# More identity products of TensorE at the beginning of a fused attention and expert layer, and score steps that carry theirs in the score bank

## What is computed

```
x = x + layernorm(attn(layernorm(x)))        # 16 heads of 8 channels, softmax over 256 keys
x = x + layernorm(ffn(layernorm(x)))
attn(x): q, k, v = split(x @ w_qkv); softmax(q k^T / sqrt(128)) v, heads joined, @ w_out
ffn(x):  logits = x @ Wr + bias; weights = softmax of the two largest of 8
         out = sum over experts of weight * ((silu(x @ Wg[e]) * (x @ Wu[e])) @ Wd[e])
         out = out + (silu(x @ Sg) * (x @ Su)) @ Sd
```

## Time and profile before

| | us |
|---|---|
| median of three executions | 377.91 |
| lowest and highest | 376.65 and 379.62 |
| profiled execution, its own time | 378.36 |
| span of its trace, first to last instruction | 376.6 |
| TensorE busy in the span | 347.9 |
| VectorE busy | 312.3 |
| ScalarE busy | 268.8 |
| GpSimd busy | 200.2 |

### The profile page before, as it was taken

The page is one execution under the profiler, slowest core; times in us unless marked ns, Lnnn a source line. Parts: engine busy times, 40 slices in busy tenths (PEclk is TensorE's granted clock), DMA queues, the critical chain, the costliest instruction groups (busy, mean ns, idle before and its releaser), DMA issues.

```text
span 376.6 us, 9905 instructions
## 1 busy us (share of the span) xinstructions
PE 347.9 (92%) x3230; PEld 220.5 (59%) x3230; DVE 312.3 (83%) x788; ACT 268.8 (71%) x511; POOL 200.2 (53%) x518
## 2 busy tenths in 40 slices
PE   6986898899999999999998999999999999998892
PEld 6854444455465657574756565665665556666672
DVE  8498498978989999998997979989998996767661
ACT  5643668788887886877888887787669868964522
POOL 5623134305372584466666455765355648867644
PEclk9899899999999999999999999999999999999998
DMA  2457946716468466367265574734664241222210
GB/s 83 120 136 159 199 98 160 167 39 151 131 157 184 119 167 156 99 145 184 52 190 119 148 168 128 172 100 132 146 150 107 61 127 58 78 71 73 58 30 29
DMA packets 59921, 45.64 MB, mean 121 GB/s; under 512 B 8966, under 2 KB 56966, under 8 KB 59870
## 3 DMA queue, kind: packets, MB, share of 16 engines
q1 hardware_dynamic: 59870, 45.00, 48.6%
HBM read 26.69 MB, written 17.81 MB: 118 GB/s over the span
## 4 chain that ended last, share of the span: by engine, by line
PE 46%; POOL 15%; issue 13%; DVE 9%; ACT 6%; DMA 6%; SPq 4%; POOLq 1%; DVEq 0%; ACTq 0%
PE pvp L648 9%; PE bank_d L818 7%; PE sc L632 6%; PE bank_d L802 6%; PE sc L617 4%; DVE mx L997 4%; PE bank_d L803 4%; POOL hidden L1206 4%; POOL rstd L1139 3%; PE bank_a L701 3%; DMA qs<-mT 2%; ACT pr L846 2%; PE bank_d L775 1%; SPq L534 1%; DMA rwb<-rw_dram 1%
## 5 line engine op out<-in xcount | busy, mean ns | idle before, releaser
L997 DVE TENSOR_REDUCE mx<-sc 128x4 f32<-128x1024 f32 x128 | 154.0, 1218 | 20.1 <-PE sc L617 18.7
L846 ACT ACTIVATE pr<-sc 128x1024 f32<-128x1024 f32 x128 | 130.5, 1024 | 25.5 <-PE sc L632 24.2
L648 PE MATMUL pvp<-pr,va 128*32 128x256 f32 x1024 | 68.4, 385 | 0.0
L802 PE MATMUL bank_d<-x3T,wg_sb 128*128 128x256 f32 x160 | 54.8, 424 | 3.2 <-DVE hidden L1095 2.8
L632 PE MATMUL sc<-qs,ks 51*128 51x256 bf16 x512 | 50.2, 277 | 6.6 <-DMA qs<-mT 4.3
L617 PE MATMUL sc<-ks,qs 48*128 48x256 bf16 x512 | 49.4, 274 | 3.1 <-DMA ks<-qk_dram 1.0
L1206 POOL TENSOR_TENSOR hidden<-hidden,rwb 128x256 f32<-128x256 f32 x60 | 42.8, 728 | 16.4 <-DMA rwb<-rw_dram 16.4
L803 PE MATMUL bank_d<-x3T,wu_sb 128*128 128x256 f32 x160 | 47.7, 380 | 0.0
L1139 POOL TENSOR_TENSOR rstd<-vareps,mhalf 128x2 f32<-128x2 f32 x64 | 44.5, 695 | 0.0
L929 ACT ACTIVATE th<-bank_d 128x256 f32<-128x256 f32 x80 | 30.4, 382 | 16.7 <-PE bank_d L803 15.7
L648 PEld LDWEIGHTS pvp<-pr,va 128*32 128x32 f32 x1024 | 26.7, 109 | 25.4 <-issue 13.1
(11 more groups left out here) (113 smaller groups left out, 488.6 us busy)
## 6 DMA issues: line engine op xcount, KB each, us to landing
rwb<-rw_dram SPq DMA_DIRECT2D x30, 256.0 KB, 4.3
qk_dram<-parts SPq DMA_DIRECT2D x30, 192.0 KB, 2.6
qs<-qk_dram SPq DMA_DIRECT2D x30, 192.0 KB, 4.6
ks<-qk_dram SPq DMA_DIRECT2D x30, 192.0 KB, 4.9
qk_dram<-parts SPq DMA_DIRECT2D x30, 128.0 KB, 2.6
pv_dram<-pv_sb SPq DMA_DIRECT2D x14, 256.0 KB, 2.3
x_sb<-in_L_attn_x_dram SPq DMA_DIRECT2D x16, 128.0 KB, 2.7
out_dram<-x SPq DMA_DIRECT2D x16, 128.0 KB, 1.9
```

The costliest lines, as they stand in the source:

```text
L648: mm = pe.matmul(pvp[32 * j:32 * j + 32, g, :], values[:, X * c + 4 * g + j, 32 * tt:32 * tt + 32], pr[:, k, c * N:(c + 1) * N], start=(tt ...
L802: pe.matmul(bank_d[bank][:, 0:N], wg_sb[:, ORDER[n], :], x3T[b % 2][:], start=True, stop=True)
L846: nc.scalar.activation(pr[:, 2 * s:2 * s + 2, :].rearrange("p k n -> p (k n)"), sc[PAIR["s2", b, s]][:].rearrange("p u c n -> p (u c n)"), ...
L997: nc.vector.tensor_reduce(mx[b % 2][:, :, :, s].rearrange("p c u -> p u c"), sc[PAIR["s1", b, s]][:], AX.X, ALU.max).then_inc(max_done, 1)
```

## The change

The table `FILL` is rewritten, and a second table `FILL_SCORES` takes all products that stand ahead of score steps. In the old tables there are 39 products, in the new two 38 and 32, together 70, so that by the tables 31 are added. The order of the steps is kept.

What changes beside the numbers is the place. Ahead of a score step the products used to run before every wait of the step, into `bank_d[1]`. Now the step first waits for its score bank (`turn(sc_empty[pair])`), then runs its products into that score bank, then waits for what else it needs (the layout of queries and keys, the maxima), and then runs its own four matmuls over the same bank.

```diff
 FILL = {
-    "maxT": {0: 9},
-    "qk": {0: 1},
-    "s1_3": {0: 2},
-    "s1_4": {0: 2, 1: 1},
-    "s1_5": {0: 2, 2: 1},
-    "s2_0": {0: 2},
-    "s2_4": {0: 2, 1: 1},
-    "s2_5": {0: 1},
-    "sel1": {0: 2},
-    "xT": {0: 12, 3: 1},
+    "maxT": {0: 10, 1: 1}, "qk": {0: 2, 3: 1}, "sel1": {0: 2}, "v": {1: 1, 3: 1}, "xT": {0: 18, 3: 2},
+}
+FILL_SCORES = {
+    ("s1", 0, 3): 2, ("s1", 0, 4): 3, ("s1", 0, 5): 2, ("s1", 1, 0): 4, ("s1", 1, 3): 1, ("s1", 1, 4): 1,
+    ("s1", 2, 5): 1, ("s1", 3, 6): 1, ("s2", 0, 0): 8, ("s2", 0, 4): 2, ("s2", 0, 5): 1, ("s2", 1, 0): 4,
+    ("s2", 1, 2): 1, ("s2", 1, 4): 1,
 }
...
+            def fill_scores(kind, b, s, pair):
+
+                for _ in range(FILL_SCORES.get((kind, b, s), 0)):
+                    pe.matmul(sc[pair][:, 0, 0, 0:P], ident[:], ident[:], start=True, stop=True)
+
             def s1(b, s):
 
+                pair = PAIR["s1", b, s]
+                turn(sc_empty[pair])
+                fill_scores("s1", b, s, pair)
                 if b and s == 0:
                     pe.wait_ge(qk_stacked[b % 2], landed1(4, b))
...
-                pair = PAIR["s1", b, s]
-                turn(sc_empty[pair])
                 q, k = qs[b % RING], ks[:, b % RING]
...
             def s2(b, s):
+                pair = PAIR["s2", b, s]
+                turn(sc_empty[pair])
+                fill_scores("s2", b, s, pair)
                 if s == 0:
                     pe.wait_ge(max_stacked[b % 2], landed(2, b))
                     if b == 0:
                         pe.wait_ge(minus_load, DMA * 2)
-                pair = PAIR["s2", b, s]
-                turn(sc_empty[pair])
```

## The result

The changed kernel takes 383.49 us in the median of four executions (382.95 to 384.67), before 377.28 us beside it; the ratio is 1.0178, 95% interval 1.0133 to 1.0223. Unchanged and run again in another set it took 384.56 us against 378.49, ratio 1.0164 (1.0122 to 1.0207). I had forecast 375.5 us, in a range of 373.7 to 378.8. A ratio counts only executions within 1.5% of the fastest of their kernel, while a median is of all of them; since before spreads from 371.9 to 385.7 us, it loses many of its slower ones, and a ratio can be nearer to one than the medians beside it.

The account below looks back on a forecast made before the run. Three falls of TensorE's clock behind idle time were taken as all that added products could win, at most 5.1 us. Terms -1.4 - 1.05 - 1.3 + 1.1 = -2.65 us gave a forecast of 375.5 us, range 373.7 to 378.8.

Parts of the forecast that it names:

- Part 4: Products moved behind the wait on a busy bank, at score steps: costs 1.1 us in sum, bounds 0 and 1.5.
- Part 2: First-pass scores to maxT, batch 0 beside batches 1 and 3: added products fit or are covered, cost 0, else 0.4 us.
- part 3: Eight products ahead of s2_0 of batch 0: cost 0, bound 0.2; kept-up clock gains 1.05 us, bounds 0 and 1.7.
- Part 1: Products added ahead of the first transposition and qk: cost 0, other bound 1.1 us; clock gain 1.4 us, bounds 0 and 1.7.
- Part 5: Third fall of the clock, 73 to 78 us: it goes too, gaining 1.3 us, bounds 0 and 1.7.
- Carried rigidly to the end: From some 80 us on, no product added and order unchanged: whatever is won or lost by then reaches the end unaltered.
- The slower rival: Three low clock stretches remain before 80 us, at other places, and part 4's delays stay: 379.5 us, chance 0.10.

Follow-up runs that it names:

- e6: e1 with twelve products ahead of the first transposition and one ahead of the first qk, as before the change; 374.52 us, ratio 0.9973 to before.
- e8: e6 unaltered, run again for a second trace; 374.61 us, ratio 0.9932 to before.
- e1: Changed kernel, all 70 products kept, those ahead of score steps back in bank_d[1] ahead of every wait; 379.60 us, ratio 1.001 to before.
- e3: Changed kernel with twelve products ahead of the first transposition and one ahead of the first qk, as before; 379.82 us, ratio 1.0062 to before.
- e4: Changed kernel without its products behind busy banks; 376.54 us, ratio 0.9972 to before.
- after again: The changed kernel unaltered, run again for a second trace; 384.56 us, ratio 1.0164 to before.
- e1 again: e1 unaltered, run again for a second trace; 380.62 us, ratio 1.003 to before.
- e2: The 39 products of before, those ahead of score steps moved behind the bank wait into the score bank; 381.85 us, ratio 1.0109 to before.
- e5: Before with twelve more products in one lump ahead of the x3T step of batch 0, near 71 us; 379.91 us, ratio 0.9975 to before.
- e9: e6 with 28 instructions of semaphore waits behind the twelve products, ahead of the first transposition; 379.23 us, ratio 1.0012 to before.

## Why the prediction was wrong

The table has a two by two in it, in medians:

| | 12 products at the start | 18 |
|---|---|---|
| old place | 374.5, 374.6 (e6, e8) | 379.6, 380.6 (e1) |
| new place | 379.8 (e3) | 383.5, 384.6 (after) |

The place costs 5.2 us in the first column and 3 to 5 us in the second, the seven products 5 to 6 us in the first row and 4 to 5 us in the second; without either, the added products win 3.4 to 5.3 us on before in medians, 1.0 to 2.6 us by the ratios. My forecast of 2.65 us lies between these two; I had the place and the seven products wrong. Against my sum the trace of after is 4.6 us behind at 79 us (+1.95 in place of -2.65) and loses another 4.4 us from there to the end.

- **Part 4, the price behind a busy bank: mis-sized.** I took 0.22 us a product and 1.1 us in all. Measured is 0.64 for the two ahead of `s2_4` and 0.42 where there is one. I dropped the 0.2 us that a group takes before its first product counts, which the idle time had hidden before, though the earlier trace rows has it as the 0.275 us from start to end. And I called places free that are not: `s1_5` of batch 2 (+0.37) and `s2_4` of batch 1 (+0.41) had one product before too, but inside the wait, and the four products ahead of `s2_0` of batch 1 cost 0.23 us in after and 0.65 in e4. Together the lag grew by 2.9 us from 43 to 71 us. The rule I cited of the Trainium skill ("TensorE: Matmul & The Clock Gate", Part 2, matmuls stay in program order) was borne out: idle, product, score, in that order.
- **Part 2, the first pass of batch 0: failed.** I had VectorE's 1.15 us a bank cover the groups, at a cost of 0, or 0.4 us at most. On TensorE `s1_3` with its two products lost 0.64 us (lag -0.49 to +0.15 at 22.14 us) and `s1_4` another 0.14, and the maxima of batch 0 came out 0.14 us late where the start had put them 0.49 us ahead. VectorE in after has an idle time of 0.42 us ahead of a maximum at 27.24 us:

```profile
27.24 1.23 DVE L1000 TENSOR_REDUCE mx<-sc 128x4 f32<-128x1024 f32 x1 [0.42 <-PE sc L619]
```

  Its like is not in before, where three maxima run there without a pause, nor in e1. The slack that I counted on, that of the SP queue, did hold: it issues the maxima of batch 0 at 32.67 us in after and at 32.25 in after again, with the cast over at 32.09 and 32.13, and `s2_0` has the same lag in both (+0.57 and +0.61). The loss went another way, over TensorE: the late maxima put the first `maxT` at 31.41 us (31.28 before), behind it stand the four products of `s1_0` of batch 1, and its scores start at 32.71 (32.59 before). From there it goes into part 3.
- **Part 1, the start: the bound, not the forecast.** The eighteen products took until 8.56 us and the first transposition came 0.81 us late. Their MATMUL instructions start 0.21 us apart at first and 0.11 us apart later, and when they change is luck: the last at 0.21 starts at 7.22 us in after, 5.30 in before, 4.23 in e1 and 6.37 in e1 again. Here the eighteen in after, then in e1:

```profile
1.51 7.05 PE L658 MATMUL bank_d<-ident 128*128 128x128 f32 x36 [1.51 <-POOL ident L1125]
```

```profile
1.51 5.62 PE L658 MATMUL bank_d<-ident 128*128 128x128 f32 x36 [1.51 <-POOL ident L1125]
```

  e1 with the same eighteen had 0.00 and 0.47. The clock then gave back what I said: from 7.59 to 15.42 the lag fell by 1.30, 1.29, 1.24 and 1.29 us in after twice and e1 twice (forecast 1.4). But it did not take the six products: twelve were enough to pass 9 us without a fall in seven of nine traces (not in before and e2), eighteen in five of five.
- **Part 3: the gain there and above the forecast, the cost of 0 wrong.** From 38.10 to 43.07 the lag fell by 1.53 us in after and in e1 (forecast 1.05). The added products also kept the clock up here: it fell between 36 and 47 us in all four traces with two of them (before twice, e2, e5) and in none of the ten with eight. But in after they now wait for a maximum first, which I had left out, and hold the scores back to 38.67 us; in e1 `s2_0` starts at 36.58, where I had it (36.7).

```profile
36.69 2.05 PE L600 MATMUL sc<-ident 128*128 128x128 f32 x16 [0.32 <-DVE mx L1000]
38.67 0.39 PE L635 MATMUL sc<-qs,ks 51*128 51x256 bf16 x4
```

- **Part 5, the third fall: wrong in after, right in e1.** After has it at 75.6 to 79 us in both traces, behind idle times of 0.36 and 0.34 us. e1 does without it and wins 1.48 us (forecast 1.3).
- **"Carried rigidly to the end": the step that failed most.** I read the part behind 80 us as one chain that shifts as a whole. The landing of a write near 190 us moved against it by 1.6 us (4.06 to 5.70), because 31 products lengthened the stream of TensorE's instructions and a fetch of its code fell into that write. TensorE idled 1.0 us more for it, and with the fall of the clock that followed, 1.5 us, 2.5 us of after's 6.3 lie there. The prediction has no term for a transfer's landing; of the other 1.9 us behind 79 us, 0.5 us lie where the late read near 290 us (e9) makes TensorE wait, and the rest stays open.
- The slower rival, at 379.5 us and a chance of 0.10, named the right sign and one of the causes, the delays of part 4. Its other condition, three low stretches before 80 us, is not met: after has one. With the delays at 2.9 in place of 1.1 us and the 2.5 us near 200 us its sum would be 383.8, near the 383.5 measured; since its condition failed, that is partly luck.

## What to carry to other kernels

A product that keeps TensorE's clock up is free only ahead of the wait that makes the idle time; behind it, it costs a start of 0.2 us more than its own time, and each place counts. Instructions added to TensorE's stream move its later fetches of code against the data transfers, so a change at 5 us can cost 5 us at 200: look at the landing times of the transfers on the critical path in both traces before blaming the edit. And where time is partly luck of the clock, compare the starts of the same matmuls in two traces, which agree within some hundredths of a microsecond until a wait, a landing or the clock differs.

## What the runs showed of the hardware

- Twenty-eight instructions that do nothing, in idle time, made the kernel slower by 4.6 us (379.23 against 374.61), with 6.8 us of low clock in its trace that neither trace of the kernel without them has.
- A write of 256 KB landed in 5.70 to 6.28 us in the six traces where a 16 KB fetch of code started 3.25 to 3.66 us behind its issue, and in 4.06 to 4.93 us in the other eight; a read near 290 us shows the same (5.91 to 6.36 against 4.99 to 5.41 us until its use) with the fetch at 3.19 to 3.56 us.
- The granted clock fell behind idle times of 1.2 to 2.8 us with TensorE at work on both sides, and also behind shorter ones: 0.36 and 0.34 us near 75 us (before, after twice, e3), 0.74 and 0.90 us at 46 us in e2. It did not fall at every such time: in after it stayed up behind the 0.74 and 0.90 us near 45 us, in e9 behind 2.65 us at 197 us, and in e1 again behind 2.94 us at 199 us.
- Between executions of before, low stretches differ in number and place; the 98 with a granted clock on record gave times of 371.9 to 385.7 us, and a line fitted through them rises by 0.39 us for each us of low clock, which is worked out from the mean granted clock of each (correlation 0.84).
